# Cross attention with a running softmax denominator: groups of four probability tiles instead of three, the row of maxima in the denominators' bank, and the output projection in other slots

## The reference, cut to what matters

```python
def _L0_xattn_ref(hidden_states, memory_keys, memory_values, attention_mask, Wq, Wout, ln_gamma, ln_beta):
    x = (hidden_states - mu) * rsqrt(var + 1e-5) * ln_gamma + ln_beta     # (32, 56, 512)
    Q = split_heads(x @ Wq.T)            # 32 heads of 16
    K = split_heads(memory_keys)         # the context itself, (32, 1500, 512)
    V = split_heads(memory_values)       # the same context
    scores = einsum('bhsd,bhtd->bhst', Q, K) * 16 ** -0.5
    probs = softmax(where(mask, scores, -inf), axis=-1)
    attn = einsum('bhst,bhtd->bhsd', probs, V)       # then back to (32, 56, 512)
    return hidden_states + attn @ Wout.T
```

## Time and profile before

| what | us |
|---|---|
| median of three runs | 1541.06 |
| the three runs | 1544.28, 1531.91, 1541.06 |
| the profiled execution, its own time | 1538.26 |
| its span, from the first to the last instruction | 1536.5 |
| mean granted TensorE clock over the span | 0.974 of 2.4 GHz |

### The profile page before, as it was taken

The page is one execution under the profiler, slowest core; times in us unless marked ns, Lnnn a source line. Parts: engine busy times, 40 slices in busy tenths (PEclk is TensorE's granted clock), DMA queues, the critical chain, the costliest instruction groups (busy, mean ns, idle before and its releaser), DMA issues.

```text
span 1536.5 us, 66930 instructions
## 1 busy us (share of the span) xinstructions
PE 1421.8 (93%) x30464; PEld 1029.0 (67%) x30464; DVE 1081.2 (70%) x3356; ACT 754.6 (49%) x623; POOL 1121.8 (73%) x403
## 2 busy tenths in 40 slices
PE   6989899999999999999999999999999999999996
PEld 4336667676676767767676766767676666777675
DVE  5557677777777676777777767777777777777730
ACT  2125455555545454554545555555555555555553
POOL 1008787877787786788877777887878778787785
PEclk8999999999999999999999989999999999999998
DMA  9204444435444343544444444544444444444320
GB/s 290 70 32 167 146 148 148 159 134 180 157 162 153 136 155 126 179 156 160 158 156 149 147 147 160 165 149 155 162 147 151 154 165 162 149 154 153 125 84 8
DMA packets 39164, 224.94 MB, mean 146 GB/s; under 512 B 4546, under 2 KB 4578, under 8 KB 26882
## 3 DMA queue, kind: packets, MB, share of 16 engines
q1 hardware_dynamic: 38882, 220.68, 42.8%
HBM read 216.90 MB, written 3.77 MB: 144 GB/s over the span
## 4 chain that ended last, share of the span: by engine, by line
PE 73%; DVE 13%; ACT 7%; issue 5%; POOL 1%; DMA 1%; SPq 0%; ACTq 0%; DVEq 0%; POOLq 0%
PE ps L239 19%; PE ps L278 17%; PE ps L293 16%; DVE masked L327 10%; PE ps L307 7%; ACT probs L362 6%; PE ps L270 5%; PE ps L255 5%; PE ps L653 4%; DVE den_inv L351 2%; ACT sums L612 1%; DVE tile_max L327 1%; DMA probs<-in_x 1%; POOL sums L408 1%; DVE neg_max L336 0%
## 5 line engine op out<-in xcount | busy, mean ns | idle before, releaser
L327 DVE CUSTOM_DVE_ANT_0 masked<-ps,mask_tile 112x500 bf16<-112x500 f32 x1536 | 982.2, 674 | 359.5 <-PE ps L239 344.3
L362 ACT ACTIVATE probs<-ps,mask_bias 125x1792 f32<-125x1792 f32 x384 | 673.9, 1755 | 654.1 <-PE ps L278 645.4
L408 POOL TENSOR_TENSOR sums<-probs 125x1792 f32<-125x1792 f32 x128 | 511.2, 3994 | 334.5 <-ACT probs L362 334.5
L412 POOL TENSOR_TENSOR sums<-sums,probs 125x1792 f32<-125x1792 f32 x128 | 511.3, 3994 | 55.4 <-ACT probs L362 48.5
L239 PE MATMUL ps<-kT,qdb 32*112 32x500 bf16 x1536 | 464.4, 416 | 49.0 <-DVE tile_max L327 43.8
L278 PEld LDWEIGHTS ps<-qd,kT 32*125 32x125 f32 x12288 | 441.8, 187 | 12.3 <-issue 10.6
L278 PE MATMUL ps<-qd,kT 32*125 32x112 f32 x12288 | 441.4, 273 | 8.9 <-issue 8.9
L293 PE MATMUL ps<-probs,v 125*32 125x112 f32 x12288 | 377.6, 263 | 4.4 <-issue 3.6
L293 PEld LDWEIGHTS ps<-probs,v 125*32 125x32 f32 x12288 | 314.2, 111 | 69.1 <-issue 38.2
L239 PEld LDWEIGHTS ps<-kT,qdb 32*112 32x112 bf16 x1536 | 164.9, 124 | 219.1 <-DVE tile_max L327 153.6
L270 PE MATMUL ps<-max_rows,ones_row 4*125 4x448 bf16 x1536 | 189.1, 394 | 16.1 <-ACT probs L362 12.4
(11 more groups left out here) (45 smaller groups left out, 236.1 us busy)
## 6 DMA issues: line engine op xcount, KB each, us to landing
kT<-in_kt SPq DMA_DIRECT2D x96, 1000.0 KB, 6.2
v<-in_ctx SPq DMA_DIRECT2D x96, 1000.0 KB
mask_tile<-mask_add SPq DMA_DIRECT2D x32, 328.1 KB, 15.4
x_res<-in_x SPq DMA_DIRECT2D x16, 224.0 KB, 15.3
out<-result SPq DMA_DIRECT2D x16, 224.0 KB, 14.9
probs<-in_x SPq DMA_DIRECT2D x14, 224.0 KB, 8.9
v<-in_wq_t SPq DMA_DIRECT2D x1, 1024.0 KB, 5.7
woutT<-in_wout_t SPq DMA_DIRECT2D x1, 1024.0 KB, 20.6
```

What stands on the lines that cost most here:

```text
L327: nc.vector.tensor_tensor_reduce(out=masked[0:PAIR_Q, t % 2, :], in0=bank[0:PAIR_Q, 0:KEYS], in1=mask_tile[0:PAIR_Q, b % 2, KEYS * c:KEYS ...
L362: nc.scalar.activation(probs[0:LANES, k % PROBS], ps[0:LANES, 0:TILES_R, 0:BANK_Q], ACT.Exp, bias=mask_bias[0:LANES, n:n + 1], scale=SCALE ...
L408: nc.gpsimd.tensor_tensor(total, probs[0:LANES, slot % PROBS], probs[0:LANES, (slot + 1) % PROBS], ALU.add).then_inc(summed, 1)
L412: nc.gpsimd.tensor_tensor(total, total, probs[0:LANES, (slot + 2) % PROBS], ALU.add).then_inc(summed, 1)
```

## The change

Each group of denominators has four slots instead of three, so that there are three groups a batch and nine additions on GpSimd where there were eight. `sum_three` becomes `add_slot`, and `make_qd`, `add_heads`, `divide_heads` and `make_qdb` stand between single additions. TensorE's halves of a group stand at slots 6, 7, 10, 11 and, for the batch before, 2 and 3. The turned rows of maxima go to free columns of bank 5, beside the denominators, by a plain matmul with the identity; they leave the ring and have a semaphore of their own (`rows_turned`). The start flag clears the accumulate state of a whole bank, so that matmul has it only for batch 0, and the next denominators wait at slot 11 until ScalarE has read the rows. The projection's quarters move to slots 8 and 9 of the even batch and 0 and 1 of the odd one.

```diff
+GROUP = 4
+SUMS = SLOTS // GROUP
+ADDS = SUMS * (GROUP - 1)
-OUT_AT = [(0, 10), (1, 1), (1, 3), (1, 4)]
-DIVIDE_AT = 1
+OUT_AT = [(0, 8), (0, 9), (1, 0), (1, 1)]
...
 def slot_others(b, k):
-    units = [("rows", b + 1)] if k == ROWS_SLOT and b + 1 < BATCH else []
-    if (b % 2, k) in OUT_AT and b > 1:
-        units += [("out", b // 2 - 1, OUT_AT.index((b % 2, k)))]
-    return units
+    return [("out", b // 2 - 1, OUT_AT.index((b % 2, k)))] if (b % 2, k) in OUT_AT and b > 1 else []
...
+        rows_bank = ps[:, 5, BLOCKS * QUERIES:BLOCKS * QUERIES + PAIR_Q]
...
-        def turn_rows(pe, unit):
-            bank = ring_bank(pe, unit)
-            pe.wait_ge(neg_ready, unit[1] + 1)
-            nc.tensor.transpose(bank[:, 0:PAIR_Q], neg_max[0:PAIR_Q].rearrange("p r n -> p (r n)"),
-                                ident[0:PAIR_Q, 0:PAIR_Q]).then_inc(ring_filled, 1)
+        def turn_rows(pe, b):
+            wait_over(pe, rows_taken, b)
+            pe.wait_ge(neg_ready, b + 1)
+            nc.tensor.matmul(rows_bank, neg_max[0:PAIR_Q].rearrange("p r n -> p (r n)"), ident[0:PAIR_Q, 0:PAIR_Q],
+                             start=(b == 0), stop=True, skip_group_check=True).then_inc(rows_turned, 1)
...
         def add_denominators(pe, b, j, e):
             if e == 0:
-                pe.wait_ge(summed, 2 * (SUMS * b + j) + 2)
+                pe.wait_ge(summed, ADDS * b + (GROUP - 1) * (j + 1))
...
         def exp_slot(act, b, k):
             if n >= PROBS:
-                act.wait_ge(summed, 2 * ((n - PROBS) // 3) + (1 if (n - PROBS) % 3 < 2 else 2))
+                act.wait_ge(summed, (GROUP - 1) * ((n - PROBS) // GROUP) + max((n - PROBS) % GROUP, 1))
...
         def spread_rows(act, b):
-            act.wait_ge(ring_filled, filled_past(("rows", b)))
+            act.wait_ge(rows_turned, b + 1)
...
+        def add_slot(pool, b, a):
+            j, m = a // (GROUP - 1), a % (GROUP - 1) + 1
+            slot, total = SLOTS * b + GROUP * j + m, sums[0:LANES, (SUMS * b + j) % 2]
+            if m == 1:
+                wait_over(pool, den_done, SUMS * b + j - 1)
+                before = probs[0:LANES, (slot - 1) % PROBS]
+            else:
+                pool.wait_ge(summed, ADDS * b + a)
+                before = total
+            pool.wait_ge(exped, slot + 1)
+            nc.gpsimd.tensor_tensor(total, before, probs[0:LANES, slot % PROBS], ALU.add).then_inc(summed, 1)
...
-                for j in range(SUMS):
-                    sum_three(pool, b, j)
+                for a in range(ADDS):
+                    add_slot(pool, b, a)
...
-                    if j == 0 and b < end:
+                    if a == 0 and b < end:
                         make_qd(pool, b + 1)
-                    if j == 0 and b > 0:
+                    if a == 0 and b > 0:
                         add_heads(pool, b - 1)
-                    if j == DIVIDE_AT and b > 0:
+                    if a == 2 and b > 0:
                         divide_heads(pool, b - 1)
-                    if j == 1 and b + 2 < BATCH:
+                    if a == 4 and b + 2 < BATCH:
                         make_qdb(pool, b + 2)
...
-                    if k >= 5 and k % 3 != 1:
-                        add_denominators(pe, b, (k - 5) // 3, (k - 5) % 3)
-                    elif k in (0, 2, 3) and b > 0:
-                        add_denominators(pe, b - 1, (k + SLOTS - 5) // 3, (k + SLOTS - 5) % 3)
+                    if k == ROWS_SLOT + 1 and b < end:
+                        pe.wait_ge(rows_taken, b + 2)
+                    if k >= 6 and (k - 6) % GROUP < 2:
+                        add_denominators(pe, b, (k - 6) // GROUP, (k - 6) % GROUP)
+                    elif k in (2, 3) and b > 0:
+                        add_denominators(pe, b - 1, SUMS - 1, k - 2)
...
+                    if k == ROWS_SLOT and b < end:
+                        turn_rows(pe, b + 1)
                     for unit in slot_others(b, k):
-                        if unit[0] == "rows":
-                            turn_rows(pe, unit)
-                        else:
-                            project_out(pe, unit)
+                        project_out(pe, unit)
             pe.wait_ge(exped, BATCH * SLOTS)
             times_values(pe, end, SLOTS - 1)
-            add_denominators(pe, end, SUMS - 2, 1)
             for e in range(2):
                 add_denominators(pe, end, SUMS - 1, e)
```

More of the change, by code:

```diff
@@ L28 @@
 PROBS = 4
-SUMS = SLOTS // 3
+GROUP = 4
+SUMS = SLOTS // GROUP
+ADDS = SUMS * (GROUP - 1)
 INVERT_AT = [(3, 3), (4, 0), (4, 2), (4, 3)]
@@ L55, in slot_others @@
 def slot_others(b, k):
-    units = [("rows", b + 1)] if k == ROWS_SLOT and b + 1 < BATCH else []
-    if (b % 2, k) in OUT_AT and b > 1:
-        units += [("out", b // 2 - 1, OUT_AT.index((b % 2, k)))]
-    return units
+    return [("out", b // 2 - 1, OUT_AT.index((b % 2, k)))] if (b % 2, k) in OUT_AT and b > 1 else []
 FIRST_TILES = [("tile", 0, t) for t in range(MAX_TILES)] + [("tile", 1, t) for t in range(AHEAD)]
-RING = FIRST_TILES + [("rows", 0)]
+RING = FIRST_TILES[:]
 RING += [unit for b in range(BATCH) for k in range(SLOTS) for unit in slot_tiles(b, k) + slot_others(b, k)]
@@ L68 @@
 RING_AT = {unit: n for n, unit in enumerate(RING)}
-TAKEN_AT = {unit: n for n, unit in enumerate(unit for unit in RING if unit[0] != "rows")}
 def build(nc, x, kt, ctx, mask_lanes, mask_rows, wq_t, wout_t, gamma, beta, out):
@@ L160, in build @@
         neg_ready = sem("neg_ready")
+        rows_turned = sem("rows_turned")
         ring_filled = sem("ring_filled")
@@ L185, in wait_taken @@
         def wait_taken(eng, unit):
-            if unit[0] == "rows":
-                eng.wait_ge(rows_taken, unit[1] + 1)
-            else:
-                eng.wait_ge(ring_taken, TAKEN_AT[unit] + 1)
+            eng.wait_ge(ring_taken, RING_AT[unit] + 1)
         def bank_of(unit):
@@ L264, in begin_scores @@
             if k == 0:
-                wait_taken(pe, ("rows", b))
+                pe.wait_ge(rows_taken, b + 1)
                 pe.wait_ge(qd_ready, b + 1)
@@ L305, in add_denominators @@
             for r in range(TILES_R):
-                own_q = sums[0:LANES, j % 2, r, :].rearrange("p (g e q) -> p g e q", g=BLOCKS, e=2)[:, :, e, :]
+                own_q = sums[0:LANES, (SUMS * b + j) % 2, r, :].rearrange("p (g e q) -> p g e q", g=BLOCKS, e=2)[:, :, e, :]
                 mm = nc.tensor.matmul(den[ROW * r:ROW * (r + 1), :, :], ones[0:LANES, e, :], own_q,
@@ L334, in take_max @@
             if b > 0:
-                dve.wait_ge(ring_filled, filled_past(("rows", b - 1)))
+                dve.wait_ge(rows_turned, b)
             nc.vector.tensor_reduce(neg_max[0:PAIR_Q, :, 0:BLOCKS],
@@ L379, in spread_rows @@
             for g in range(BLOCKS):
-                ins = nc.scalar.activation(max_rows[:, b % 2, g, :], bank_of(("rows", b))[:, 0:PAIR_Q], ACT.Copy,
+                ins = nc.scalar.activation(max_rows[:, b % 2, g, :], rows_bank, ACT.Copy,
                                            scale=own_block[:, g:g + 1])
@@ L401, in make_qd @@
             spread_q(pool, qd, b).then_inc(qd_ready, 1)
-        def sum_three(pool, b, j):
-            n, slot = SUMS * b + j, SLOTS * b + 3 * j
-            total = sums[0:LANES, j % 2]
-            wait_over(pool, den_done, n - 1)
-            pool.wait_ge(exped, slot + 2)
-            nc.gpsimd.tensor_tensor(total, probs[0:LANES, slot % PROBS], probs[0:LANES, (slot + 1) % PROBS],
-                                    ALU.add).then_inc(summed, 1)
-            pool.wait_ge(summed, 2 * n + 1)
-            pool.wait_ge(exped, slot + 3)
-            nc.gpsimd.tensor_tensor(total, total, probs[0:LANES, (slot + 2) % PROBS], ALU.add).then_inc(summed, 1)
+        def add_slot(pool, b, a):
[9 more added lines that the diff above has]
+            nc.gpsimd.tensor_tensor(total, before, probs[0:LANES, slot % PROBS], ALU.add).then_inc(summed, 1)
         def add_heads(pool, b):
@@ L590, in _ @@
                     for unit in slot_others(b, k):
-                        if unit[0] == "out":
-                            take_unit(dve, unit)
+                        take_unit(dve, unit)
             for g in range(BLOCKS):
@@ L661, in _ @@
             pe.wait_ge(consts, CONSTS)
-            turn_rows(pe, ("rows", 0))
+            turn_rows(pe, 0)
             pe.wait_ge(wout_landed, 16)
```

2 lines of the change are left out of this document (1 added, 1 removed).

## The result

| what | before | changed |
|---|---|---|
| median of the runs, us | 1538.28 (4 runs, 1531.91 to 1544.28) | 1497.32 (4 runs, 1495.71 to 1499.33) |
| ratio, with its 95% interval | | 0.9735 [0.969, 0.978] |
| span of the profiled execution, us | 1536.5 | 1494.0 |
| mean granted clock of that execution | 0.974 | 0.987 |

The changed kernel is 41 us faster, 2.7%. The direction was right; the forecast, 1520 in a range from 1492 to 1545, had less than half of the gain.

A forecast was written before the change was run, and what follows sets the result against it. TensorE at first sight (93% busy), but really each slot's excess over a 3.24 us floor. Per pair +0.20 - 0.2 - 0.8 = -0.8, 16 pairs -13, clock -6, end +1: -18, from 1538.3 to 1520; range 1492 to 1545.

The forecast's parts named there:

- The loop and its floor of 3.24 us: In every slot on ScalarE, an exponential of 1.75 us and a 1.48 us wait for scores make 3.24; never shorter.
- The projection's quarters, +0.20 a pair: Four quarters cost 3.60 us a pair where they stood, 3.80 in slots without denominators: net +0.20 a pair.
- The rows leaving the ring: In slot 10 the tile behind the rows loses its wait, -0.50 us; the plain matmul's second pass adds +0.14.
- The groups of four: Denominator halves leave slots 0, 5, 8, 9 and enter 7: -0.2 us a pair; in slot 10 +0.40 and -0.45.
- Slot 10 as a whole: -0.50 + 0.14 + 0.40 - 0.45 = -0.4 us a batch, 4.65 to 4.25 in both batches; -0.8 a pair.
- The clock: Cold time costs 26 us; 6 of it goes, as slots 10 lose their long wait; ends 0 and -20.
- GpSimd, at no cost: GpSimd, 93% of a batch with nine additions, still delivers in time, 1.3 us to spare at slot 6: no cost.
- rival C: GpSimd late for the first group at slot 6, from 1.3 us of lateness: +1.6 us a batch, 1589 us; chance 0.10.
- VectorE beside GpSimd: VectorE's tiles, 615 to 681 ns with one input in PSUM, are not blocked by GpSimd's longer work: zero.
- The end: In the last batch the final additions, in a row from slot 9, end at 14.1 instead of 13.3: +0.9 us.
- Rival A: Backlog vanishes: slots 5 to 7 and 10 reach the floor, clock keeps up; 1465 at most, about 1500; chance 0.23.
- Rival B: Nothing won: denominators' half takes in slots 10 and 7 what the ring gives; 1526 to 1550, say 1536; chance 0.25.

The follow-up runs named there:

- rows_groups: Kernel before with the rows out of the ring and groups of four, the projection's quarters left where they were; 1491.33 us, ratio 0.970.
- proj_only: Kernel before with only the projection's quarters moved to slots 8 and 9 of even and 0 and 1 of odd batches; 1529.63 us, ratio 0.997.
- rows_only: Kernel before with only the turned rows taken out of the ring, groups of three and quarters unchanged; 1503.09 us, ratio 0.978.
- groups_only: Kernel before with only groups of four, rows still in the ring and quarters where they were; 1510.35 us, ratio 0.982.
- rows_proj: Kernel before with the rows out of the ring and the quarters moved, still groups of three; 1507.94 us, ratio 0.980.
- late_max: Changed kernel with two buffers for the tile maxima, negative maxima formed after VectorE's third tile of slot 10; 1489.03 us, ratio 0.969 to the kernel before.
- gpsimd_late3: Changed kernel with three more unused 0.94 us GpSimd instructions behind the first addition of each batch; 1521.92 us.
- fill_slot10: Kernel before with four small unused bfloat16 matmuls on TensorE right after the turned rows in slot 10; 1531.72 against 1536.56 us, ratio 0.997.
- groups_proj: Kernel before with groups of four and the quarters moved, rows still in the ring; 1510.07 us, ratio 0.982.
- gpsimd_late1: Changed kernel with one more unused 0.94 us GpSimd instruction behind the first addition of each batch; 1497.22 us.

## Why the prediction was off, step by step

**The loop and its floor of 3.24 us: right.** No slot has a lower median in any kernel run here; one slot in each trace is shorter, 3.15 or 3.16. It is why a saving of 39 us of denominator matmuls has to be read slot by slot.

**The projection's quarters, +0.20 a pair: right in size.** The last step to the changed kernel (rows_groups to changed) is +0.17, and proj_only gives +0.17. But "each like slot 1 of batch 13", 0.95, was about right only in the mean (0.93): against rows_groups it is 1.22, 0.79, 0.91 and 0.78.

**The rows leaving the ring, -0.36 a batch: undersized.** It was -0.45 in an odd batch and -0.63 in an even one, -1.15 a pair by rows_only against -0.72. The step "the tile follows some 0.35 us behind the rows" came out at 0.41 with the second pass in it, so the separate +0.14 for that pass was too much by 0.08. In an even batch a quarter stands behind the rows, and it is the quarter that had to wait: in batch 14 of rows_only it follows the rows by 0.31 us where it had been 0.85, and the tile follows the quarter by 0.97 where it had been 1.06. I had carried the odd batch's number over.

**The groups of four, -0.2 a pair outside of slot 10 and about -0.1 in it: the step that failed most.** groups_only measured -0.82, and beside the rows (rows_only to rows_groups) it is -0.95. What failed is the part outside of slot 10: -0.85 where I had -0.2. Slot 5 of the even batch lost 0.32, as I had it, but slot 6 also lost, in both batches (0.12 and 0.10), and slot 9 in both (0.13 and 0.14). For the odd batches I had read slot 9 in batch 13 alone, where it stands at 3.24; the median was 3.38. The +0.1 that I had put down for slot 7 in either batch was +0.06 and +0.01. The part in slot 10 was about right, with +0.02 and +0.01: the half at 0.37 against 0.40, and against it the earlier second tile.

**Slot 10 as a whole, 4.25 in both: 3.82 and 4.33.** The slot can be cut in three at TensorE's tiles: from the exponential to the start of the second tile, from there to the third tile, and from there to the next exponential. Medians over the same batches, us, even batches first and then odd ones (medians of parts need not add up to that of the slot):

| kernel | start of second tile | second to third tile | third tile to end |
|---|---|---|---|
| before | 0.65, 0.65 | 1.26, 1.26 | 3.91, 2.85 |
| rows_only | 0.65, 0.65 | 1.26, 1.26 | 3.28, 2.40 |
| groups_only | 0.29, 0.19 | 1.63, 1.63 | 3.91, 2.85 |
| rows_proj | -0.22, 0.65 | 1.26, 1.26 | 2.40, 2.40 |
| changed | -0.22, 0.29 | 1.63, 1.63 | 2.40, 2.40 |
| late_max | -0.43, -0.21 | 1.62, 1.63 | 2.40, 2.40 |

So each term of the prediction can be seen by itself. The half costs 0.37 (I had 0.40). Leaving the ring is worth 0.45 in an odd batch, the second pass already taken off (I had 0.36). The earlier second tile is worth 0.36 in an odd batch and 0.87 in an even one, where I had 0.45 for both. The odd slot was right because two of these errors, 0.09 each, cancelled. The even one was too long by the 0.42 that its second tile came earlier than I had it; the quarter that left the slot and the ring together took 1.51, as I had it (1.16 + 0.36).

**The clock, -6: too small, by about half.** There are now 33 runs of the kernel before, from 1523.47 to 1558.92 us, with mean clocks from 0.982 down to 0.957. A straight line through them has 1303 us for one unit of mean clock, with a correlation of -0.96 (1304 and -0.92 without the three that the ratios leave out). From the mean of these 33 (0.9744) to that of the changed kernel's four runs (0.9852) this would be 14 us. At that clock the line gives 1523.5 for the kernel before, against a mean of 1497.4: the other 26 us. The slot ledger splits the gain alike: -1.93 for some 15 pairs is 29 us, -0.89 for the 14 pairs that were counted is 12. The line alone does not say which causes which, since a stall makes a run longer and can let the clock fall; in the one trace of gpsimd_late3 a wait of 1.1 us put into slot 6 has falls right behind it. But slot 10's wait is not all of it: the mean clock of the runs is 0.986 for rows_only, 0.980 for proj_only, and 0.984 for groups_only, whose slot 10 is as long as before. In the trace of groups_only the clock fell three times between the first slot and the last, never in a slot 10, where the half of denominators now stands between the waits; in that of proj_only it fell eight times, seven of them in an odd slot 10. These are single traces. Why the groups of four alone raised the clock stays open, and so does whether filling a wait does as well as removing it (fill_slot10).

**GpSimd, at no cost: right,** and the rival C had the right place, order and point from which it decides: 1.56 us of room where I had 1.3. Its size is not shown: in gpsimd_late3 only slot 6 grew by more than 0.05 us, and GpSimd's list did not set the batch. **VectorE beside GpSimd: right.** With 32 more additions VectorE's tiles have a mean of 671 ns and a maximum of 680, against 674 and 681 of before. This agrees with the rule of the Trainium skill (SBUF — State Buffer, "SBUF: two separate sides") that was weighed. **The end, +0.9: half of it.** The last addition ends 13.99 us after the exponential of slot 9 where it ended 13.16 after it, +0.83 as I had it, but from that exponential to the end of the span it is 27.2 against 26.8 us, +0.4.

**Rival A** had the right sum (about 1500), but by luck. Its clock term of 20 us is above the 12 to 14 that the two counts give, and its mechanism is not what happened: the backlog behind slot 4 is still there in part (even 5, 6 and 7 at 3.38, 3.31 and 3.38), and slot 10 isn't at the floor. **Rival B** said that the denominators' half would take back what the ring gives. The half did take its 0.37 in every slot 10, but against the kernel before the earlier second tile gave back 0.36 or more, and in slot 7 it took little: +0.07 in the even batch and +0.13 in the odd one of the changed kernel.

## What to carry to other kernels

Where two engines run in a loop with a floor, cut the time into the loop's rounds and read each round's excess over the floor; busy shares (93% before and after) say nothing. A round whose length stays the same after work was added to it has not shown that the work was free. Here a half of denominators cost its 0.37 us in every slot 10, and the round stayed at its length only where the same change let it start 0.36 earlier; so cut such a round at fixed instructions and compare the pieces, before calling a wait a cover. Read more than one round of each kind too: slot 9 of the one odd batch that I read was at the floor, and its median was not. Price each part of a change both alone and with the others. In the regular part of 86.5 us three of the four combinations were within 0.13 us of the sum of their parts, and groups_proj was 0.44 below it. Moving the quarters gained nothing that can be told from noise alone (0.997) and cost 6 us beside the other two; without it and with the maxima taken later the kernel runs in 1483.0 us, 14 us below the changed one.

## What the runs showed that was not expected

The kernel before scatters by 2.3% over its 33 runs (1523 to 1559 us), 1.3% without the three that the ratios leave out, and the scatter follows the mean granted clock, 13 us for each 0.01. The changed one scatters by 0.24% over its four runs, but four runs say little of this: gpsimd_late1, whose four runs have the same median, scatters by 0.7%. The irregular part, 2.15 us a pair of batches before, was 1.62, 1.28 and 1.09 in the one trace each of the groups, the quarters and the rows alone. In the changed kernel 0.81 of the 1.26 that are left lies in slots 8 and 9, and no run here says what causes it.
